# Layer norm by features from the fourth group on, and probabilities turned with shared corners

## The chip, the cores and the metric

One core of a Trainium2 chip runs the kernel. Its engines work in order, each from a queue of its own, and are tied by semaphores: TensorE (PE) multiplies matrices, VectorE (DVE), ScalarE (ACT) and GpSimd (POOL) work element by element, SyncE (SP) issues the transfers (DMA). Matmuls write to PSUM; POOL sees SBUF alone. The metric is the device time of one execution in microseconds.

## The reference, cut to what matters

The input x has 32 sequences of 256 tokens with 128 features.

```python
xn = (x - mean(x)) / sqrt(var(x) + 1e-5)              # over the features of a token
h = relu(xn @ nm_w1 + nm_b1);  m = h @ nm_w2 + nm_b2
q, k, v = m @ q_w + q_b, m @ k_w + k_b, m @ v_w + v_b
# token s attends to tokens s-32 .. s+32 of its sequence
attn = softmax(q k^T / sqrt(128), over that band) v
# feed-forward: 16 experts, each token uses the 8 best, weights normalised and x 2.826
y = sum_e combine_e * ((silu(xn @ w_gate_e.T) * (xn @ w_up_e.T)) @ w_down_e.T)
y += (silu(xn @ shared_gate_w.T) * (xn @ shared_up_w.T)) @ shared_down_w.T
out = x + attn + y
```

## The kernel before

The 8192 tokens are worked in 16 groups of 512 (`GROUPS`), two sequences each. Within a group 17 steps (`STEPS`) run over the shared expert and the 16 others. All large tensors are held by features: 128 features on the partitions, 512 tokens along the row. Each float32 operand is kept as a high part and a low part of a type that TensorE takes at full speed, and a product is made of three matmuls (high x high, high x low, low x high; `PAIRS3`).

Each engine's program is the same double loop, group g and slot s, written out by hand. `slot(g, par, s)` says what the engine issues there, in that order; nothing else sets the order. `when(g, s, fresh)` gives another slot in group 0. In one slot:

- PE: gate_proj of step s+1 (three matmuls), a piece of the attention (`att_early`), down of step s-3, `att_late`, up_proj of step s. gate_proj waits for the silu two steps before, up_proj for `h_lo` two steps before, since they share a PSUM bank.
- ACT: `h_hi` (high part of the product of step s-1), the silu of step s+1, a piece of the attention.
- POOL: silu of step s+1 times the routing weights (`silu_c`, from `comb_b`, the weights of all experts spread over the partitions). There is none for step 0, so slot 16 has none.
- DVE: `h_prod` of step s-1 (silu_c times the up product, in PSUM), a piece of the attention or of the routing (`att`), then `h_lo` of step s-1.

The layer norm of a group runs ahead of it. x is loaded by tokens (`load_x`, 128 tokens on the partitions, four tiles). DVE takes the moments (`moments`, `variance`; slots 12 and 14, two groups ahead), POOL the power -1/2 (`inverse_std`, slot 16), DVE subtracts and multiplies (`normalise`, four instructions in slot 0, one group ahead). PE turns the result tile by tile into PSUM (`turn` into bank[1], slot 1), ACT copies the high part from there (`xn_hi`, slot 1) and DVE subtracts it for the low part (`xn_lo`, slot 2). The gate matmuls of the routing (`gate`) need both in slot 4. x is also loaded by features as `xres` (`load_res`), for the sum at the end (`finish_group`, slot 3 of the group after).

The attention of a sequence works with two tiles of 128 queries, each of which sees a window of 160 keys (`WIN`). DVE takes the row maximum (`row_max`, slots 4 and 6), ACT the exponential, DVE multiplies by the inverse sum (`normalise_probs`, slots 6 and 8) into `prob_n`, a row of 256 keys for each tile with zeros outside the window. PE turns it (`turn_probs`, slots 7 and 9): two halves of keys by two tiles, four transposes. ACT and DVE copy the parts that are not zero (`halves`, windows of 160 queries for either half of the keys) as high and low parts (`prob_hi`, `prob_lo`), which `attend` uses in slots 13 and 14.

SP issues all transfers in its loop order: in slot 3 the store of the last output, xres and x, in slot 13 the store of the routing weights to memory (`store_comb`, which waits for DVE's last routing instruction) and their spread over the partitions in four blocks (`spread`).

Of the kernel before, what the change touches and what calls it, by code (L numbers as in the profile page):

```python
# [12 lines left out]
P = 128  # L13
# [8 lines left out]
STEPS = E + 1  # L22
HALF = 32
WIN = P + HALF
EPS = 1e-5
ROUTE_SCALE = 2.826
SCALE = float(P) ** -0.5
# [18 lines left out]
NH = 4  # L46


DVE_LO = (6, 8)


# [13 lines left out]
    return next(d for d in range(1, 2 * STEPS + 1) if order[(p - d) % (2 * STEPS)] == order[p])  # L65


def layer(nc, x, x_t, watt, watt_t, expert_bias, wexp, out_t, c_dram):
    ctx = ExitStack()
    with ctx:  # L70
        def sb(name, shape, dt=F32):
# [5 lines left out]
        def sem(name):  # L77
# [25 lines left out]
        mv = sb("mv", [P, TILES, 2])  # L103
        var_eps = sb("var_eps", [P, TILES])
        rstd = sb("rstd", [P, TILES])
        xn = sb("xn", [P, TILES, P])
        xn_t = [[sb(f"xn_hi{i}", [P, T], F32R), sb(f"xn_lo{i}", [P, T], F32R)] for i in range(2)]


# [9 lines left out]
        row_sum = sb("row_sum", [P, TILES])  # L119
        row_inv = sb("row_inv", [P, TILES])  # L120
        prob = sb("prob", [P, TILES, WIN])
        prob_n = sb("prob_n", [P, TILES, SEQ])
        p_t = [sb("p_hi", [P, NB, 2, SEQ], F32R), sb("p_lo", [P, NB, 2, WIN], F32R)]


# [30 lines left out]
        s_expw_in = [sem(f"expw_loaded{i}") for i in range(len(EXPW))]  # L156
        s_xin = [sem(f"x_loaded{i}") for i in range(2)]
        s_xres = [sem(f"xres_loaded{i}") for i in range(2)]
        s_const0 = sem("const_cleared")
        s_const1 = sem("const_band_low")  # L160
        s_const = sem("const_ready")
# [34 lines left out]
        s_y_out = sem("y_evacuated")  # L196
        s_stored = [sem(f"y_stored{i}") for i in range(2)]

        names = """bn aggr var_eps rstd xn xn_tp xn_hi xn_lo gate_mm gate_s gate_e
# [36 lines left out]
        def flat(t):  # L236
            return t[:].rearrange("p a d -> p (a d)")

        def halves(b):

            return b[:].rearrange("p (t c) -> p t c", t=2)[:, :, 0:WIN]

        @block.sync
        def _(sp):
            def load_x(g, par):
                sp.dma_start(xin[par][:], x[g * T:(g + 1) * T, :].rearrange("(a p) d -> p a d", p=P))\
                    .then_inc(s_xin[par], 16)
# [25 lines left out]
            def prologue():  # L273
                load_x(0, 0)
                sp.dma_start(att_raw[:], watt).then_inc(s_watt_in, 16)
                for i, (lo, hi) in enumerate(EXPW):
                    sp.dma_start(exp_raw[:, lo:hi, :], wexp[:, lo:hi, :]).then_inc(s_expw_in[i], 16)
                    if i == 0:
                        sp.dma_start(att_t[:], watt_t).then_inc(s_wt_in, 16)
                    if i == 1:  # L280
                        sp.dma_start(ebias[:], expert_bias.to_broadcast([P, E])).then_inc(s_ebias_in, 16)
                    if i == 2:
                        load_x(1, 1)
                load_res(0, 0)

                store_comb(0, 0)
                for c in range(1, NCHUNK):
                    spread(0, 0, c, True)

            def slot(g, par, s):  # L290
                if s == 3:
                    if not first(g):
                        store_y(g - 1, 1 - par)
                    if not last(g):
                        if not first(g):

                            sp.wait_ge(s_stored[1 - par], 8 * (g - 1 + (1 + par)))
                        load_res(g + 1, 1 - par)
                    if not last(g, 1):

                        sp.wait_ge(S["xn"], g + 1)
                        load_x(g + 2, par)
                if s == 13 and not last(g):
# [12 lines left out]
        def _(pe):  # L316
# [30 lines left out]

            def turn_probs(seq):
                dst = score_bank[seq]
                for kb in range(2):  # L350
                    for t in range(2):
                        c = kb * (SEQ - (P - HALF)) + t * P
                        done = nc.tensor.transpose(dst[:, c:c + P],  # L353
                                                   prob_n[:, 2 * seq + t, kb * P:(kb + 1) * P], ident[:])
                done.then_inc(S[f"pt{seq}"], 1)

            def attend(seq):
# [214 lines left out]
        def _(act):  # L572
# [6 lines left out]
                A(exp_w[0][:, s, :], exp_raw[:, s, :], ACT.Copy).then_inc(s_expw_hi, 1)  # L579

            def xn_hi(g, par):
                act.wait_ge(S["xn_tp"], g + 1)
                A(xn_t[par][0][:], bank[1][:], ACT.Copy).then_inc(S["xn_hi"], 1)

            def gate_exp(g):
                act.wait_ge(S["gate_s"], g + 1)
# [28 lines left out]

            def prob_hi(g, seq):
                act.wait_ge(S[f"pt{seq}"], g + 1)
                A(p_t[0][:, seq, :, 0:WIN], halves(score_bank[seq]), ACT.Copy).then_inc(S[f"p{seq}_hi"], 1)

            def gate_silu(g, par, s):  # L620
                i = (par + s) % 2
# [108 lines left out]
        def _(dve):  # L730
# [13 lines left out]
            def variance(g):  # L744
# [15 lines left out]

            def xn_lo(g, par):
                dve.wait_ge(S["xn_hi"], g + 1)
                V.tensor_tensor(xn_t[par][1][:], bank[1][:], xn_t[par][0][:].bitcast(F32), ALU.subtract)\
                    .then_inc(S["xn_lo"], 1)

            def gate_sum(g):
# [141 lines left out]
            def normalise_probs(g, seq):  # L908
# [2 lines left out]
                V.reciprocal(row_inv[:, n], row_sum[:, n]).then_inc(S[f"inv{seq}"], 1)  # L911
                dve.wait_ge(S[f"inv{seq}"], g + 1)
                for t in range(2):
                    c = t * (P - HALF)
                    done = V.tensor_scalar(prob_n[:, 2 * seq + t, c:c + WIN], prob[:, 2 * seq + t, :],
                                           row_inv[:, 2 * seq + t:2 * seq + t + 1], None, ALU.mult)
                done.then_inc(S[f"pn{seq}"], 1)

            def prob_lo(g, seq):
                dve.wait_ge(S[f"p{seq}_hi"], g + 1)  # L920
                V.tensor_tensor(p_t[1][:, seq, :, :], halves(score_bank[seq]),
                                p_t[0][:, seq, :, 0:WIN].bitcast(F32), ALU.subtract).then_inc(S[f"p{seq}_lo"], 1)

            def att(g, par, s):
                more = not last(g)
                more2 = not last(g, 1)
                if first(g):
                    fresh_att(s)
                if s == when(g, 0, 3) and more:
                    normalise(g + 1, 1 - par)  # L930
                if s == when(g, 1, 4):
                    hid_n_lo(g)
# [28 lines left out]
                if s == when(g, 12, 13) and more2:  # L961
                    moments(g + 2, par)
                if s == 14:
                    if more2:
                        variance(g + 2)
                    if more:
                        hid_lo(g + 1)
# [58 lines left out]
        def _(pool):  # L1026
# [6 lines left out]

            def inverse_std(g):
                pool.wait_ge(S["var_eps"], g + 1)
                G.tensor_tensor(rstd[:], var_eps[:], power[:], ALU.pow).then_inc(S["rstd"], 1)

            def prologue():
                G.memset(power[:], -0.5)
# [29 lines left out]
            def slot(g, par, s):  # L1069
# [16 lines left out]
                                    silu[i][:].rearrange("p (l x) -> p l x", l=2),  # L1086
                                    comb_b[:, :, s1 - 1, :], ALU.mult).then_inc(s_silu_c, 1)
                elif not last(g, 1):
                    inverse_std(g + 2)
# [42 lines left out]
```

## Time and profile before

| | us |
|---|---|
| median of 3 runs (lowest, highest) | 715.92 (715.48, 717.18) |
| the profiled execution | 715.54 |
| its span, first to last instruction | 713.4 |
| PE busy | 702.2 (98%) |
| DVE busy | 573.1 (80%) |
| ACT busy | 440.6 (62%) |
| POOL busy | 405.3 (57%) |

The span is what the profiler sees of the execution; 2.1 us lie around it. Busy time is the union of an engine's instructions. Matmuls overlap each other, so their durations do not add up to their share of the time; the distance from one start to the next does. In the rows below, a line of the code stands as L396, a tile group as ps_u<-xn_hi,exp_w_hi (written, then read), and "x4" behind a row says how many instructions it merges.

### The profile page before, as it was taken

The page shows a single profiled execution, that of the slowest core. Times are in us where ns is not written, and L with a number is a line of the kernel's source. Part 1 is how long each engine was busy: PE and PEld are TensorE (multiplying, and loading weights), DVE is VectorE, ACT ScalarE, POOL GpSimd, SP SyncE. Part 2 cuts the span into 40 slices and gives each one's busy share as a digit, 9 for nine tenths or more (in the row PEclk, how much of TensorE's full clock was granted, in tenths as well). Part 3 has the DMA queues.
Part 4 walks back from the last instruction along what each step waited for, and adds up shares of the span by engine and source line. Part 5 has one row for each costly group of instructions (what it writes and reads, how often), then busy time and mean ns, then how long its engine had stood idle before and what let it go on. Part 6 is the DMA issues. An engine that isn't in the chain of part 4 may idle for free.

```text
span 713.4 us, 10683 instructions
## 1 busy us (share of the span) xinstructions
PE 702.2 (98%) x3412; PEld 577.4 (81%) x3412; DVE 573.1 (80%) x1598; ACT 440.6 (62%) x878; POOL 405.3 (57%) x363
## 2 busy tenths in 40 slices
PE   8889999999999999999999999999999999999997
PEld 6668888888888888888888888888888888888886
DVE  6888787887878888788887878878788887878775
ACT  5766665656665576655657566566665766656573
POOL 4785665555556555666555555554656546555463
PEclk9999999999999999999999999999999999999999
DMA  7606144071621506134061421516125061430600
GB/s 260 208 0 221 62 129 154 5 247 33 206 77 46 228 10 239 45 109 175 2 236 45 178 104 35 219 30 237 46 79 203 2 236 45 150 117 8 247 0 16
DMA packets 36519, 83.67 MB, mean 117 GB/s; under 512 B 7152, under 2 KB 15600, under 8 KB 36464
## 3 DMA queue, kind: packets, MB, share of 16 engines
q1 hardware_dynamic: 36464, 83.00, 33.7%
q8 instruction: 27, 0.44, 0.3%
q14 instruction: 28, 0.23, 0.1%
HBM read 78.27 MB, written 4.72 MB: 116 GB/s over the span
## 4 chain that ended last, share of the span: by engine, by line
PE 94%; DVE 3%; ACT 2%; issue 0%; DMA 0%; POOL 0%; DVEq 0%
PE ps_y L406 26%; PE ps_u L396 26%; PE ps_g L386 26%; PE bank L321 3%; PE bank L363 3%; PE bank L344 3%; PE bank L326 2%; PE bank L353 2%; PE bank L333 2%; PE ps_y L372 1%; DVE ps_u L997 1%; DVE h_lo L1003 1%; ACT h_hi L631 0%; DMA xin<-x 0%; DVE xn L755 0%
## 5 line engine op out<-in xcount | busy, mean ns | idle before, releaser
L1085 POOL TENSOR_TENSOR silu_c<-silu,comb_b 128x512 f32<-128x512 f32 x256 | 330.7, 1294 | 291.1 <-ACT silu L623 289.5
L631 ACT ACTIVATE h_hi<-ps_u 128x512 fp32r<-128x512 f32 x272 | 162.5, 597 | 258.4 <-DVE ps_u L997 256.4
L1003 DVE TENSOR_TENSOR h_lo<-ps_u,h_hi 128x512 fp32r<-128x512 f32 x272 | 185.8, 683 | 59.7 <-ACT h_hi L631 59.5
L997 DVE TENSOR_TENSOR ps_u<-silu_c,ps_u 128x512 f32<-128x512 f32 x256 | 176.9, 691 | 44.5 <-PE ps_u L396 38.7
L623 ACT ACTIVATE silu<-ps_g 128x512 f32<-128x512 f32 x272 | 161.5, 594 | 1.7 <-PE ps_g L386 1.5
L396 PE MATMUL ps_u<-xn_hi,exp_w_hi 128*128 128x512 f32 x272 | 110.5, 406 | 4.7 <-DVE h_lo L1003 4.7
L406 PE MATMUL ps_y<-h_hi,exp_w_hi 128*128 128x512 f32 x272 | 112.6, 414 | 0.4 <-DVE h_lo L1003 0.4
L386 PE MATMUL ps_g<-xn_hi,exp_w_hi 128*128 128x512 f32 x272 | 108.1, 397 | 0.0
L386 PE MATMUL ps_g<-xn_lo,exp_w_hi 128*128 128x512 f32 x272 | 107.8, 396 | 0.0
L386 PE MATMUL ps_g<-xn_hi,exp_w_lo 128*128 128x512 f32 x272 | 107.6, 396 | 0.0
L406 PE MATMUL ps_y<-h_hi,exp_w_lo 128*128 128x512 f32 x272 | 107.5, 395 | 0.0
L396 PE MATMUL ps_u<-xn_lo,exp_w_hi 128*128 128x512 f32 x272 | 107.4, 395 | 0.0
L406 PE MATMUL ps_y<-h_lo,exp_w_hi 128*128 128x512 f32 x272 | 107.2, 394 | 0.0
L396 PE MATMUL ps_u<-xn_hi,exp_w_lo 128*128 128x512 f32 x272 | 107.2, 394 | 0.0
L396 PEld LDWEIGHTS ps_u<-xn_hi,exp_w_hi 128*128 128x128 f32 x272 | 51.3, 189 | 16.2 <-DVE h_lo L1003 6.2
L386 PEld LDWEIGHTS ps_g<-xn_hi,exp_w_hi 128*128 128x128 f32 x272 | 51.3, 188 | 12.7 <-POOL exp_w_lo L1031 0.4
L386 PEld LDWEIGHTS ps_g<-xn_hi,exp_w_lo 128*128 128x128 f32 x272 | 51.3, 189 | 12.4
L406 PEld LDWEIGHTS ps_y<-h_hi,exp_w_lo 128*128 128x128 f32 x272 | 51.1, 188 | 12.5
L396 PEld LDWEIGHTS ps_u<-xn_hi,exp_w_lo 128*128 128x128 f32 x272 | 51.0, 188 | 12.1
L386 PEld LDWEIGHTS ps_g<-xn_lo,exp_w_hi 128*128 128x128 f32 x272 | 51.1, 188 | 12.0
L396 PEld LDWEIGHTS ps_u<-xn_lo,exp_w_hi 128*128 128x128 f32 x272 | 51.4, 189 | 10.1
L406 PEld LDWEIGHTS ps_y<-h_hi,exp_w_hi 128*128 128x128 f32 x272 | 51.3, 189 | 9.6 <-DVE h_lo L1003 0.8
(146 smaller groups left out, 992.1 us busy)
## 6 DMA issues: line engine op xcount, KB each, us to landing
comb_b<-c_dram SPq DMA_DIRECT2D x63, 1024.0 KB, 8.9
xin<-x SPq DMA_DIRECT2D x16, 256.0 KB, 3.4
xres<-x_t SPq DMA_DIRECT2D x16, 256.0 KB, 2.9
out_t<-xres SPq DMA_DIRECT2D x16, 256.0 KB, 2.0
exp_raw<-wexp SPq DMA_DIRECT2D x2, 960.0 KB, 10.8
c_dram<-comb_t SPq DMA_DIRECT2D x64, 8.0 KB, 1.8
exp_raw<-wexp SPq DMA_DIRECT2D x1, 768.0 KB, 7.6
exp_raw<-wexp SPq DMA_DIRECT2D x1, 384.0 KB, 5.4
```

The costliest lines, as they stand in the source:

```text
L321: done = mm(dst[:], att_w[a][:, w, :], parts[b][:], start=n == 0, stop=n == 2)
L326: done = nc.tensor.transpose(dst[:, a * P:(a + 1) * P], src[:, a * P:(a + 1) * P], ident[:])
L344: done = mm(dst[:, t * SEQ:t * SEQ + WIN], q_t[a][:, q0:q0 + P], hid_t[b][:, k0:k0 + WIN], start=n == 0, stop=n == 2)
L363: done = mm(bank[2][:, col:col + wide], hid_n[a][:, seq * 2 + kb, :], p_t[b][:, seq, kb, 0:wide], start=kb == 0 and n == 0, stop=kb == 1 a ...
L386: done = mm(ps_g[i][:], exp_w[a][:, s, 0:P], xn_t[par][b][:], start=n == 0, stop=n == 2)
L396: done = mm(ps_u[i][:], exp_w[a][:, s, P:2 * P], xn_t[par][b][:], start=n == 0, stop=n == 2)
L406: done = mm(ps_y[:], exp_w[a][:, s, 2 * P:3 * P], h_t[i][b][:], start=s == 0 and n == 0, stop=s == STEPS - 1 and n == 2, skip_group_check= ...
L623: A(silu[i][:], ps_g[i][:], ACT.Silu).then_inc(s_silu, 1)
L631: A(h_t[hbuf(par, s)][0][:], ps_u[(par + s) % 2][:], ACT.Copy).then_inc(s_h_hi, 1)
L997: V.tensor_tensor(ps_u[i][:], src[:], ps_u[i][:], ALU.mult).then_inc(s_h, 1)
L1003: V.tensor_tensor(t[1][:], ps_u[(par + s) % 2][:], t[0][:].bitcast(F32), ALU.subtract)\
L1085: G.tensor_tensor(silu_c[i][:].rearrange("p (l x) -> p l x", l=2), silu[i][:].rearrange("p (l x) -> p l x", l=2), comb_b[:, :, s1 - 1, :], ...
```

## The change

Two parts.

Layer norm. For groups 3 to 15 (`TURNED = 3`) x is loaded by tokens (now with four neighbouring tokens on a partition) for the moments alone, and once more by features, straight into `xn`. The mean and the inverse deviation of the 512 tokens are stored to memory and read back spread over all partitions (`mom_b`, 2 x 512 per partition). POOL then subtracts the mean in two halves (slots 14 and 15) and multiplies (slot 16), two groups ahead. `xn_hi` and `xn_lo` read `xn` in SBUF. The instructions of `normalise` on DVE and of `turn` on PE are gone for these groups. The moments are taken three groups ahead in slots 12 and 13, the power goes to slot 7, `xn_lo` for all groups but the first to slot 3. SP gets load_turned in slot 5 and, in slot 8, the store of the moments, the wait for it, and the spread.

Probabilities. `prob_n` holds one row of 384 per sequence: the first tile's window in columns 0 to 159, the second's in 224 to 383. PE turns it in three blocks of 128. The middle block holds the first tile's keys 128 to 159 and the second tile's keys 96 to 127; a query of the other tile has zeros at those keys, so one block serves both windows, which now lie 224 apart.

```diff
+APART = 3 * P - WIN
+TURNED = 3
         xn = sb("xn", [P, TILES, P])
+        mom = sb("mom", [P, 2, TILES])
+        mom_b = sb("mom_b", [P, 2, T])
-        prob_n = sb("prob_n", [P, TILES, SEQ])
+        prob_n = sb("prob_n", [P, NB, 3 * P])
-        def halves(b):
-            return b[:].rearrange("p (t c) -> p t c", t=2)[:, :, 0:WIN]
+        def windows(b):
+            return b[:, 0:2 * APART].rearrange("p (t c) -> p t c", t=2)[:, :, 0:WIN]
 # SP
+            def load_turned(g):
+                if g == TURNED:
+                    sp.wait_ge(S["xn_tp"], g)
+                else:
+                    sp.wait_ge(S["xn_lo"], g)
+                sp.dma_start(flat(xn), x_t[:, g * T:(g + 1) * T]).then_inc(s_xt, 16)
+            def spread_moments(g):
+                n = g - TURNED + 1
+                sp.wait_ge(S["rstd"], g + 1)
+                sp.wait_ge(S["mean"], n)
+                sp.dma_start(st_dram.rearrange("k (p a) -> p k a", p=P), mom[:]).then_inc(s_mom_st, 16)
+                sp.wait_ge(s_mom_st, 16 * n)
+                if n > 1:
+                    sp.wait_ge(S["xn"], g)
+                sp.dma_start(mom_b[:], st_dram.rearrange("(o k) t -> o k t", o=1).to_broadcast([P, 2, T]))\
+                    .then_inc(s_mom_b, 16)
                 if s == 3: ...
+                if s == 5 and TURNED <= g + 2 < GROUPS:
+                    load_turned(g + 2)
+                if s == 8:
...
+                    if TURNED <= g + 2 < GROUPS:
+                        spread_moments(g + 2)
 # PE
             def turn_probs(seq):
                 dst = score_bank[seq]
-                for kb in range(2):
-                    for t in range(2):
-                        c = kb * (SEQ - (P - HALF)) + t * P
-                        done = nc.tensor.transpose(dst[:, c:c + P],
-                                                   prob_n[:, 2 * seq + t, kb * P:(kb + 1) * P], ident[:])
+                for n in range(3):
+                    done = nc.tensor.transpose(dst[:, n * P:(n + 1) * P], prob_n[:, seq, n * P:(n + 1) * P],
+                                               ident[:])
-                if s == when(g, 1, 5) and more:
+                if s == when(g, 1, 5) and g + 1 < TURNED:
                     pe.wait_ge(S["xn"], g + 2)
 # DVE
             def variance(g):
...
+                if g > TURNED:
+                    dve.wait_ge(S["rstd"], g)
                 V.tensor_scalar(var_eps[:], mv[:, :, 1], EPS, None, ALU.add).then_inc(S["var_eps"], 1)
+                if g >= TURNED:
+                    n = g - TURNED
+                    if n > 0:
+                        dve.wait_ge(s_mom_st, 16 * n)
+                    V.tensor_copy(mom[:, 0, :], mv[:, :, 0]).then_inc(S["mean"], 1)
-                if s == when(g, 0, 3) and more:
+                if s == when(g, 0, 3) and g + 1 < TURNED:
                     normalise(g + 1, 1 - par)
-                if s == when(g, 2, 6) and more:
+                if s == when(g, 3, 6) and more:
                     xn_lo(g + 1, 1 - par)
+                if s == 12 and TURNED < g + 3 < GROUPS:
+                    moments(g + 3, 1 - par)
+                if s == 13: ... variance(g + 3)
 # POOL
             def inverse_std(g):
                 pool.wait_ge(S["var_eps"], g + 1)
+                if g > TURNED:
+                    pool.wait_ge(s_mom_st, 16 * (g - TURNED))
+                dst = rstd[:] if g < TURNED else mom[:, 1, :]
+                G.tensor_tensor(dst, var_eps[:], power[:], ALU.pow).then_inc(S["rstd"], 1)
+            def centre(g, half):
+                n = g - TURNED + 1
+                if half == 0:
+                    pool.wait_ge(s_xt, 16 * n)
+                    pool.wait_ge(s_mom_b, 16 * n)
+                c = slice(half * T // 2, (half + 1) * T // 2)
+                G.tensor_tensor(flat(xn)[:, c], flat(xn)[:, c], mom_b[:, 0, c], ALU.subtract)\
+                    .then_inc(S[f"centred{half}"], 1)
+            def normalise(g):
+                n = g - TURNED + 1
+                pool.wait_ge(S["centred0"], n)
+                pool.wait_ge(S["centred1"], n)
+                G.tensor_tensor(flat(xn), flat(xn), mom_b[:, 1, :], ALU.mult).then_inc(S["xn"], 1)
                 elif not last(g, 1):
+                    if g + 2 < TURNED: inverse_std(g + 2)
+                    else: normalise(g + 2)
+                if TURNED <= g + 2 < GROUPS:
+                    if s == 7: inverse_std(g + 2)
+                    if s == 14: centre(g + 2, 0)
+                    if s == 15: centre(g + 2, 1)
```

## Rows read from the trace of the kernel before

**Rows 1.** The page: busy time and share of each engine, instructions.

```profile
PE 702.2 (98%) x3412; PEld 577.4 (81%) x3412; DVE 573.1 (80%) x1598; ACT 440.6 (62%) x878; POOL 405.3 (57%) x363
```

**Rows 2.** Engines' busy time in one group's stretch; PEclk is the granted clock.

```profile
79.30:122.30 43.00, 43.00 (x211) 35.53 (x211) 35.09 (x100) 26.68 (x54) 24.28 (x21) 1.00 0.35 117
```

**Rows 3.** Timeline of POOL: start, length, what, [idle before <-who ended it].

```profile
331.27 1.35 POOL L1066 TENSOR_SCALAR mask_k<-mask,key_term 128x160 f32<-128x160 f32 x2
...
343.44 2.54 POOL L1085 TENSOR_TENSOR silu_c<-silu,comb_b 128x512 f32<-128x512 f32 x2 [4.31 <-ACT silu L623]
346.81 1.28 POOL L1085 TENSOR_TENSOR silu_c<-silu,comb_b 128x512 f32<-128x512 f32 x1 [0.82 <-ACT silu L623]
...
362.38 1.30 POOL L1085 TENSOR_TENSOR silu_c<-silu,comb_b 128x512 f32<-128x512 f32 x1 [1.46 <-ACT silu L623]
363.64 1.04 POOL L1036 TENSOR_TENSOR rstd<-var_eps,power 128x4 f32<-128x4 f32 x1
367.76 1.29 POOL L1085 TENSOR_TENSOR silu_c<-silu,comb_b 128x512 f32<-128x512 f32 x1 [3.09 <-ACT silu L623]
...
386.48 2.54 POOL L1085 TENSOR_TENSOR silu_c<-silu,comb_b 128x512 f32<-128x512 f32 x2 [4.31 <-ACT silu L623]
```

**Rows 4.** The waits: in total, times, longest.

```profile
PE ps_u L396 <- DVE h_lo L1003: 4.7, 4, 1.6
```

**Rows 5.** Timeline of PE, turning of xn in group 7.

```profile
326.07 0.60 PE L326 MATMUL bank<-ident,xn 128*128 128x128 f32 x4
...
326.74 0.40 PE L406 MATMUL ps_y<-h_lo,exp_w_hi 128*128 128x512 f32 x1
```

**Rows 6.** Groups of instructions: busy us, mean ns | idle before.

```profile
L326 PE MATMUL bank<-ident,xn 128*128 128x128 f32 x60 | 9.0, 272 | 0.0
```

**Rows 7.** Timeline of PE, a turning of probabilities.

```profile
304.30 0.60 PE L353 MATMUL bank<-ident,prob_n 128*128 128x128 f32 x4
...
304.97 0.39 PE L396 MATMUL ps_u<-xn_lo,exp_w_hi 128*128 128x512 f32 x1
```

**Rows 8.** Timeline of group 0, DVE, POOL and PE.

```profile
42.96 1.57 DVE L915 TENSOR_SCALAR prob_n<-prob,row_inv 128x160 f32<-128x160 f32 x2
...
43.42 1.01 POOL L1031 TENSOR_TENSOR exp_w_lo<-exp_raw,exp_w_hi 128x384 fp32r<-128x384 f32 x1
...
44.45 0.68 DVE L1003 TENSOR_TENSOR h_lo<-ps_u,h_hi 128x512 fp32r<-128x512 f32 x1
...
45.19 0.50 PE L396 MATMUL ps_u<-xn_hi,exp_w_hi 128*128 128x512 f32 x1 [1.12 <-DVE h_lo L1003]
...
52.73 0.50 PE L396 MATMUL ps_u<-xn_hi,exp_w_hi 128*128 128x512 f32 x1 [1.40 <-DVE h_lo L1003]
```

**Rows 9.** Timeline of DVE in group 7, slots 3, 5 and 8.

```profile
332.45 0.69 DVE L1003 TENSOR_TENSOR h_lo<-ps_u,h_hi 128x512 fp32r<-128x512 f32 x1 [0.66 <-ACT h_hi L631]
...
335.93 0.70 DVE L997 TENSOR_TENSOR ps_u<-silu_c,ps_u 128x512 f32<-128x512 f32 x1 [0.83 <-PE ps_u L396]
...
345.64 0.65 DVE L915 TENSOR_SCALAR prob_n<-prob,row_inv 128x160 f32<-128x160 f32 x2
...
346.53 0.67 DVE L1003 TENSOR_TENSOR h_lo<-ps_u,h_hi 128x512 fp32r<-128x512 f32 x1
```

**Rows 10.** Timeline of PE in group 7, slots 4 and 9.

```profile
333.45 0.18 PE L333 MATMUL bank<-gate_w,xn_hi 128*128 128x32 f32 x1
...
347.69 0.48 PE L396 MATMUL ps_u<-xn_hi,exp_w_hi 128*128 128x512 f32 x1
```

**Rows 11.** The page: transfers, KB each, median us to landing.

```profile
comb_b<-c_dram SPq DMA_DIRECT2D x63, 1024.0 KB, 8.9
...
c_dram<-comb_t SPq DMA_DIRECT2D x64, 8.0 KB, 1.8
```

**Rows 12.** Timeline of group 0, slot 2, POOL and DVE.

```profile
21.85 1.01 POOL L1036 TENSOR_TENSOR rstd<-var_eps,power 128x4 f32<-128x4 f32 x1
...
22.07 0.68 DVE L823 TENSOR_TENSOR hid_lo<-hid,hid_hi 128x512 fp32r<-128x512 f32 x1
```

More of the change, by code:

```diff
@@ L65, in hdist, with layer @@
     return next(d for d in range(1, 2 * STEPS + 1) if order[(p - d) % (2 * STEPS)] == order[p])
-def layer(nc, x, x_t, watt, watt_t, expert_bias, wexp, out_t, c_dram):
+def layer(nc, x, x_t, watt, watt_t, expert_bias, wexp, out_t, c_dram, st_dram):
     ctx = ExitStack()
@@ L158, in layer @@
         s_xres = [sem(f"xres_loaded{i}") for i in range(2)]
+        s_xt = sem("x_t_loaded")
+        s_mom_st = sem("moments_stored")
+        s_mom_b = sem("moments_spread")
         s_const0 = sem("const_cleared")
@@ L197, in layer @@
         s_stored = [sem(f"y_stored{i}") for i in range(2)]
-        names = """bn aggr var_eps rstd xn xn_tp xn_hi xn_lo gate_mm gate_s gate_e
+        names = """bn aggr var_eps rstd mean centred0 centred1 xn xn_tp xn_hi xn_lo gate_mm gate_s gate_e
             gate_1 score select top8 rest weight wsum winv comb comb_t
@@ L245, in load_x @@
             def load_x(g, par):
-                sp.dma_start(xin[par][:], x[g * T:(g + 1) * T, :].rearrange("(a p) d -> p a d", p=P))\
-                    .then_inc(s_xin[par], 16)
+                rows = x[g * T:(g + 1) * T, :]
+                rows = rows.rearrange("(a p) d -> p a d" if g < TURNED else "(p a) d -> p a d", p=P)
+                sp.dma_start(xin[par][:], rows).then_inc(s_xin[par], 16)
+            def load_turned(g):
[14 more added lines that the diff above has]
+                    .then_inc(s_mom_b, 16)
             def load_res(g, par):
@@ L298, in slot @@
                         load_res(g + 1, 1 - par)
-                    if not last(g, 1):
+                    if first(g):
                         sp.wait_ge(S["xn"], g + 1)
                         load_x(g + 2, par)
+                    elif not last(g, 2):
+                        if g + 1 < TURNED:
+                            sp.wait_ge(S["xn"], g + 2)
+                        else:
+                            sp.wait_ge(S["bn"], g + 2)
+                        load_x(g + 3, 1 - par)
+                if s == 5 and TURNED <= g + 2 < GROUPS:
+                    load_turned(g + 2)
+                if s == 8:
+                    if first(g):
+                        sp.wait_ge(S["xn"], g + 2)
+                        load_x(g + 3, 1 - par)
+                    if TURNED <= g + 2 < GROUPS:
+                        spread_moments(g + 2)
                 if s == 13 and not last(g):
@@ L581, in xn_hi @@
             def xn_hi(g, par):
-                act.wait_ge(S["xn_tp"], g + 1)
-                A(xn_t[par][0][:], bank[1][:], ACT.Copy).then_inc(S["xn_hi"], 1)
+                if g < TURNED:
+                    act.wait_ge(S["xn_tp"], g + 1)
+                else:
+                    act.wait_ge(S["xn"], g + 1)
+                A(xn_t[par][0][:], bank[1][:] if g < TURNED else flat(xn), ACT.Copy).then_inc(S["xn_hi"], 1)
             def gate_exp(g):
@@ L617, in prob_hi @@
                 act.wait_ge(S[f"pt{seq}"], g + 1)
-                A(p_t[0][:, seq, :, 0:WIN], halves(score_bank[seq]), ACT.Copy).then_inc(S[f"p{seq}_hi"], 1)
+                A(p_t[0][:, seq, :, 0:WIN], windows(score_bank[seq]), ACT.Copy).then_inc(S[f"p{seq}_hi"], 1)
             def gate_silu(g, par, s):
@@ L762, in xn_lo @@
                 dve.wait_ge(S["xn_hi"], g + 1)
-                V.tensor_tensor(xn_t[par][1][:], bank[1][:], xn_t[par][0][:].bitcast(F32), ALU.subtract)\
+                src = bank[1][:] if g < TURNED else flat(xn)
+                V.tensor_tensor(xn_t[par][1][:], src, xn_t[par][0][:].bitcast(F32), ALU.subtract)\
                     .then_inc(S["xn_lo"], 1)
@@ L913, in normalise_probs @@
                 for t in range(2):
-                    c = t * (P - HALF)
-                    done = V.tensor_scalar(prob_n[:, 2 * seq + t, c:c + WIN], prob[:, 2 * seq + t, :],
+                    c = t * APART
+                    done = V.tensor_scalar(prob_n[:, seq, c:c + WIN], prob[:, 2 * seq + t, :],
                                            row_inv[:, 2 * seq + t:2 * seq + t + 1], None, ALU.mult)
@@ L920, in prob_lo @@
                 dve.wait_ge(S[f"p{seq}_hi"], g + 1)
-                V.tensor_tensor(p_t[1][:, seq, :, :], halves(score_bank[seq]),
+                V.tensor_tensor(p_t[1][:, seq, :, :], windows(score_bank[seq]),
                                 p_t[0][:, seq, :, 0:WIN].bitcast(F32), ALU.subtract).then_inc(S[f"p{seq}_lo"], 1)
@@ L960, in att @@
                     route_weights(g + 1, 1 - par)
-                if s == when(g, 12, 13) and more2:
-                    moments(g + 2, par)
+                if g == TURNED - 2:
+                    if s == 4:
+                        moments(g + 2, par)
+                    if s == 5:
+                        variance(g + 2)
+                if s == 12 and TURNED < g + 3 < GROUPS:
+                    moments(g + 3, 1 - par)
+                if s == 13:
+                    if first(g):
+                        moments(g + 2, par)
+                    elif g + 3 < GROUPS:
+                        variance(g + 3)
                 if s == 14:
-                    if more2:
+                    if first(g):
                         variance(g + 2)
@@ L1035, in inverse_std @@
                 pool.wait_ge(S["var_eps"], g + 1)
-                G.tensor_tensor(rstd[:], var_eps[:], power[:], ALU.pow).then_inc(S["rstd"], 1)
+                if g > TURNED:
[15 more added lines that the diff above has]
+                G.tensor_tensor(flat(xn), flat(xn), mom_b[:, 1, :], ALU.mult).then_inc(S["xn"], 1)
             def prologue():
@@ L1088, in slot @@
                 elif not last(g, 1):
-                    inverse_std(g + 2)
+                    if g + 2 < TURNED:
+                        inverse_std(g + 2)
+                    else:
+                        normalise(g + 2)
+                if TURNED <= g + 2 < GROUPS:
+                    if s == 7:
+                        inverse_std(g + 2)
+                    if s == 14:
+                        centre(g + 2, 0)
+                    if s == 15:
+                        centre(g + 2, 1)
                 if s == when(g, 2, 5):
@@ L1128 @@
     c_dram = nc.dram_tensor("c_dram", (2, 2 * E, 2, P), F32, kind="Internal").ap()
-    layer(nc, *args, out_t, c_dram)
+    st_dram = nc.dram_tensor("st_dram", (2, T), F32, kind="Internal").ap()
+    layer(nc, *args, out_t, c_dram, st_dram)
     r = run_bass_kernel_spmd(nc, [arrays], core_ids=[0])
```

## The prediction

> **What bounds the kernel now.** I read the page first. TensorE is busy for 98% of the span, while VectorE, the next engine, has 80% [rows 1]. So I ask where TensorE ever waits. From 79.30 to 122.30 us, which is one group of the loop, it is busy for 43.00 of 43.00 us at full clock [rows 2], and the same place of two groups lies 386.48 - 343.44 = 43.04 us apart [rows 3]: a stream of matmuls without a hole. The waits agree: the largest of TensorE is up_proj behind VectorE's h_lo, 4 times in the whole run, 4.7 us together [rows 4]. Hence an instruction taken out of TensorE's stream in a full group shortens the span by the time for which it holds the stream, as long as no other engine becomes late. The busy durations are not that time, since matmuls overlap; the distance between starts is.
>
> **What a transpose holds.** From the start of the four transposes of xn to the start of the second matmul behind them it is 326.74 - 326.07 = 0.67 us [rows 5]: the four, and the distance from one matmul to the next. The row of the transposes tells the two apart: 0.60 us for four, less the 0.272 us that one lasts [rows 6], is 0.33 us for three pitches, or 0.109 each. Four hold 0.44 us, and the 0.23 us left of the 0.67 is the matmul's. The turning of the probabilities gives 304.97 - 304.30 = 0.67 again, so I use 0.109 per transpose there too [rows 7].
>
> **The change, part by part.**
>
> *xn by features, no turning.* Groups 3 to 15, that is 13, lose four transposes each: 52 x 0.109 = 5.67 us. They all stand in slot 1 of groups 2 to 14, which are full ones.
>
> *Corners in one piece.* Each of the 32 turnings issues three transposes in place of four: 32 x 0.109 = 3.49 us. But group 0's two savings disappear in its stalls: TensorE waits 1.12 us for h_lo just ahead of the first and 1.40 us behind the second [rows 8], so that VectorE sets the pace there. I count 30: 3.27 us. The copies of the windows keep their size and number, so ACT and VectorE have the same work on them.
>
> *VectorE.* It loses the four multiply-subtracts of slot 0 and gains one copy of four columns. Slot 0 is not what TensorE waits for, so this is worth nothing by itself. The low part of xn moves from slot 2 to slot 3, where VectorE waited 0.66 us for ACT [rows 9]: it fits. It now reads two SBUF tensors. If it had to wait out the whole pair of mask instructions on POOL (1.35 us from 331.27, [rows 3]) it would end near 331.27 + 1.35 + 0.69 = 333.31; the gate matmuls that need it start at 333.45 [rows 10] or, with TensorE 0.44 us ahead, at 333.01. So its price is between 0 and 0.3 us a group. I take 0, nearest to the row of 0.66: only a loss of both handovers gives the other end. The moments move from slot 14 to 13 and belong to a later group; slot 14 is relieved by as much.
>
> *POOL.* New are two half-tile subtractions and one multiplication, and the power moves from slot 16 to slot 7. A full-tile product takes at most 1.30 us, and I bound a half by it. The first half comes into the 1.46 us of idle time ahead of 362.38; the product there ends at 363.68, then the second half and the multiplication end by 363.68 + 1.3 + 1.3 = 366.3, while the next product starts at 367.76 [rows 3]. Hidden, with 1.5 us to spare. The power in slot 7 starts behind the pair of products that ends at 343.44 + 2.54 = 345.98 and ends 1.04 us later, at 347.02. The next product started at 346.81, so it is 0.2 us late, which its reader, in VectorE's next slot, does not notice.
>
> *The trip through memory.* It begins when the power ends (347.02) and must be over for slot 14, about 361: 14 us. From below it is bounded by two transfers of the 8 KB kind, 3.6 us; from above by 1.8 + 8.9 us, the latter for a spread of twice the size [rows 11]. 10.7 is less than 14, so it costs nothing; I would guess 7. If the cover were gone, each microsecond beyond it and beyond POOL's 1.46 us of idle time would stop POOL. On SP's queue the store, the wait for it and the spread now stand ahead of the store of the routing weights. That one waits for VectorE's routing work, which ends in slot 11, four slots after the power, so SP is back by then; if the spread's bytes delay it by a microsecond, the first block of the spread weights, used at 367.76 [rows 3], still comes in time by about as much.
>
> **What is late next.** Behind ACT's two table loads VectorE runs late through slots 8 to 12, and this is the one place with little room. In group 7 h_lo of step 7 ends at 346.53 + 0.67 = 347.20 and TensorE starts the up_proj that needs it at 347.69: 0.49 us [rows 9, 10]. In group 0, where TensorE does wait, it starts at 45.19 after h_lo's end at 44.45 + 0.68 = 45.13 [rows 8]: 0.06 is the price of the semaphore, so 0.43 is to spare. That room is measured from slot 5, where VectorE still waits for TensorE (0.83 us at 335.93, [rows 9]), so all that is saved before it moves both engines. Between it and these slots only the two turnings of probabilities are shorter, 0.22 us. There remain 0.21 us: nothing stalls, but little would make it.
>
> **The sum.** 715.54 (the profiled execution: a span of 713.4 and 2.1 around it) - 5.67 - 3.27 = 706.60. The median of the runs shown is 0.38 us above that execution, so 707.0 us.
>
> **The rivals.**
>
> *A, the power holds VectorE's second multiply.* In slot 8 the two multiplies of the probabilities start at 345.64, the first waits for POOL's products to end at 345.98, and both are done at 346.29 [rows 3, 9]. Now the power is queued right behind those products. Group 0 has the same pattern: two multiplies take 1.57 us together instead of 0.65, because a product of 384 columns that started on POOL at 43.42 came between them; they end at 44.53, 0.10 us after it [rows 8]. If the power did that, the pair would end at 345.98 + 1.04 + 0.10 = 347.12, 0.83 us late, of which 0.21 is covered: 0.62 us in each of groups 1 to 13, 8.1 us, which gives 714.7, or 715.1 as a median. Against it: at 22.07 VectorE's hid_lo, which reads two SBUF tensors, starts 0.22 us into a power of 1.01 us and takes 0.68, no longer than its like [rows 12]. A power reads only eight columns and seems to hold nothing while it computes. Chance 0.13. The Trainium skill, "SBUF — State Buffer", section "Who interferes with whom", says that a VectorE instruction in a two-port mode and a GpSimd one exclude each other, and that the later one "fully blocks". By that rule the power holds the multiply for its whole length and the time is this rival's. The trace agrees for instructions that stream their columns; for the power it speaks against it, as far as a two-input instruction can tell.
>
> *B, part of the room is used up.* Delays of 0.1 to 0.4 us beyond the 0.21 in slots 8 to 12, from a multiply held while the power reads or a low part of xn held in slot 3 (0.3 us at most): over 13 groups 1.3 to 5 us, so 708.3 to 712. Chance 0.09.
>
> *C, the moments come late: slower.* POOL executes in order. Its subtraction in slot 14 waits for the spread, and behind it stands the product for step 16 that VectorE multiplies with. A trip longer than 14 us plus the 1.46 us of idle time delays it. To be slower by over 0.3% (about what a measurement of this kernel can tell from no change, 2.15 us) each of 13 groups would have to lose (8.9 + 2.15) / 13 = 0.85 us, so the trip would have to last over 16.3 us; at 16.5 us each loses 1.04 us and the time is 707.0 + 13.5 = 720.5. For it speaks that the store writes runs of 16 bytes, which no row shows; against it the bound of 10.7. Chance 0.03.
>
> *D, the turnings of xn were free,* because a hidden wait takes their place, for instance finish_group in slot 3. Then 3.27 us alone are saved: 712.6. Against it stands that no row shows a wait of TensorE there. Chance 0.03.
>
> **How the numbers follow.** The forecast has 0.72, with 706.2 to 708 as its own range. The range for 8 in 10 takes in B and leaves out A: 705.9 to 712. Faster by over 0.3% means under 713.8: 0.72 + 0.09 + 0.03 (D) + 0.01 of A = 0.85. Same: the rest of A, 0.12. Slower: C, 0.03.
>
> **What would show it.** A period of 43.04 - 0.44 - 0.22 = 42.38 us between groups, with TensorE busy in all of it, shows both savings right; over 42.5 us makes the forecast wrong. A multiply of about 1 us in slot 8, and an up_proj of slot 9 that waits for h_lo, is A. POOL waiting for a DMA in slot 14 is C. TensorE waiting in slots 2 to 4 is D or the held low part of xn. The distance between starts around the three transposes should be 0.67 - 0.11 = 0.56 us.

## The result, and the profile after

| | us |
|---|---|
| changed kernel, median of 4 runs (lowest, highest) | 704.49 (703.62, 705.41) |
| kernel before beside it, median | 715.80 |
| ratio | 0.984, 95% interval 0.9824 to 0.9856 |
| profiled execution, its span | 703.68, 701.9 |

The kernel became 11.3 us faster by the medians. The time lies 2.5 us below the forecast of 707.0 and below its range, which began at 705.9. The medians mix two kinds of execution 1.5 to 1.7 us apart, with a mean granted clock of 0.994 to 0.995 or of 0.996 to 0.998, and leave out one execution of e1_before_pad32 that took 1786.93 us. The two profiled executions, with 0.998 and 0.997, are 715.54 - 703.68 = 11.9 us apart. What was said of the transposes and of the waits holds in the main; what is missing in the sum is a gain of TensorE in matmuls that the change does not touch.

The page of the changed kernel, busy time by engine, and its transfers:

```profile
PE 690.3 (98%) x3328; PEld 568.6 (81%) x3328; DVE 564.3 (80%) x1559; ACT 439.2 (63%) x878; POOL 446.0 (64%) x402
...
comb_b<-c_dram SPq DMA_DIRECT2D x63, 1024.0 KB, 8.7
mom_b<-st_dram SPq DMA_DIRECT2D x13, 512.0 KB, 3.8
```

The instructions of TensorE fell by 84, the 52 and 32 transposes. POOL has 41 us more, VectorE 9 less [rows 1]. Now a whole group (columns as in [rows 2]):

```profile
121.20:163.40 42.20, 42.20 (x207) 34.93 (x206) 34.47 (x96) 26.64 (x54) 27.42 (x25) 1.00 0.41 138
```

TensorE is busy in all of it, as before, at the full level of its clock (1.00). Its timeline in slots 5 to 9 of group 7 (start, length, what):

```profile
332.83 0.40 PE L444 MATMUL ps_u<-xn_hi,exp_w_hi 128*128 128x512 f32 x1
...
337.00 0.40 PE L444 MATMUL ps_u<-xn_hi,exp_w_hi 128*128 128x512 f32 x1
...
342.21 0.49 PE L401 MATMUL bank<-ident,prob_n 128*128 128x128 f32 x3
342.46 0.48 PE L444 MATMUL ps_u<-xn_hi,exp_w_hi 128*128 128x512 f32 x1
342.77 0.40 PE L444 MATMUL ps_u<-xn_lo,exp_w_hi 128*128 128x512 f32 x1
```

From the start of the three transposes to the start of the second matmul behind them it is 342.77 - 342.21 = 0.56 us, where with four it was 0.67 [rows 7]: the 0.11 of the sum. The first two rows are what the sum lacks. Between them lie two steps, 18 matmuls of 512 columns and nothing else: 4.17 us. Before, the same place reads

```profile
337.80 0.40 PE L396 MATMUL ps_u<-xn_hi,exp_w_hi 128*128 128x512 f32 x1
...
342.00 0.39 PE L396 MATMUL ps_u<-xn_hi,exp_w_hi 128*128 128x512 f32 x1
```

4.20 us. On the mean an untouched matmul starts between 1 and 2 ns sooner, and a group has 153 in its steps alone. The gain is not spread evenly. The largest share lies at one place of the nine, between the second and the third matmul of gate_proj; before, and after:

```profile
340.83 0.40 PE L386 MATMUL ps_g<-xn_lo,exp_w_hi 128*128 128x512 f32 x1
341.07 0.40 PE L386 MATMUL ps_g<-xn_hi,exp_w_lo 128*128 128x512 f32 x1
...
335.85 0.39 PE L434 MATMUL ps_g<-xn_lo,exp_w_hi 128*128 128x512 f32 x1
336.07 0.39 PE L434 MATMUL ps_g<-xn_hi,exp_w_lo 128*128 128x512 f32 x1
```

Over the full groups this distance has a mean of 233 ns before and of 226 after; the other eight changed by between -4 and +1 ns each, 6 ns less in all. VectorE and POOL in slots 7 and 8 of the same group:

```profile
339.88 0.70 DVE L1067 TENSOR_TENSOR ps_u<-silu_c,ps_u 128x512 f32<-128x512 f32 x1 [0.27 <-POOL silu_c L1173]
340.48 0.16 DVE L971 RECIPROCAL row_inv<-row_sum 128x2 f32<-128x2 f32 x1
340.67 0.66 DVE L975 TENSOR_SCALAR prob_n<-prob,row_inv 128x160 f32<-128x160 f32 x2
341.26 0.39 DVE L846 MAX8 top<-select 128x8 f32<-128x16 f32 x4
341.57 0.67 DVE L1073 TENSOR_TENSOR h_lo<-ps_u,h_hi 128x512 fp32r<-128x512 f32 x1
```

```profile
338.47 2.55 POOL L1173 TENSOR_TENSOR silu_c<-silu,comb_b 128x512 f32<-128x512 f32 x2 [4.32 <-ACT silu L674]
340.97 1.05 POOL L1109 TENSOR_TENSOR mom<-var_eps,power 128x4 f32<-128x4 f32 x1
...
354.40 1.30 POOL L1173 TENSOR_TENSOR silu_c<-silu,comb_b 128x512 f32<-128x512 f32 x1 [0.83 <-ACT silu L674]
355.66 0.73 POOL L1117 TENSOR_TENSOR xn<-xn,mom_b 128x256 f32<-128x256 f32 x1
357.07 1.30 POOL L1173 TENSOR_TENSOR silu_c<-silu,comb_b 128x512 f32<-128x512 f32 x1 [0.68 <-ACT silu L674]
358.32 0.74 POOL L1117 TENSOR_TENSOR xn<-xn,mom_b 128x256 f32<-128x256 f32 x1
359.21 1.29 POOL L1124 TENSOR_TENSOR xn<-xn,mom_b 128x512 f32<-128x512 f32 x1
...
380.64 2.56 POOL L1173 TENSOR_TENSOR silu_c<-silu,comb_b 128x512 f32<-128x512 f32 x2 [4.32 <-ACT silu L674]
```

The power starts at 340.97, before the second multiply of the pair could, and the pair takes 0.66 as before. h_lo ends at 342.24 and up_proj starts at 342.46: of 0.49 us, 0.22 are left. The same place of two groups is 380.64 - 338.47 = 42.17 us apart; before it was 43.04, and the sum said 42.38.

### The profile page after: what moved, and what is told of

It reads as the page before. It is cut to its first block, busy times and chain, and to the rows that moved or that the text cites. A ratio compares the mean times of both kernels' runs of the same rounds, so it can differ in the third digit from the quotient of the medians.

```text
span 701.9 us, 10616 instructions
## 1 busy us (share of the span) xinstructions
PE 690.3 (98%) x3328; PEld 568.6 (81%) x3328; DVE 564.3 (80%) x1559; ACT 439.2 (63%) x878; POOL 446.0 (64%) x402
## 4 chain that ended last, share of the span: by engine, by line
PE 93%; DVE 3%; ACT 3%; issue 1%; DMA 0%; POOL 0%; DVEq 0%
PE ps_u L444 26%; PE ps_y L454 26%; PE ps_g L434 26%; PE bank L371 3%; PE bank L411 3%; PE bank L394 3%; PE bank L383 2%; PE ps_y L420 1%; PE bank L401 1%; PE bank L376 1%; DVE ps_u L1067 1%; DVE h_lo L1073 1%; ACT h_hi L682 1%; DMA xin<-x 0%; DVE xn L814 0%
## 5 line engine op out<-in xcount | busy, mean ns | idle before, releaser
L434 PE MATMUL ps_g<-xn_lo,exp_w_hi 128*128 128x512 f32 x272 | 106.0, 390 | 0.0
```

The costliest lines, as they stand in the source:

```text
L434: done = mm(ps_g[i][:], exp_w[a][:, s, 0:P], xn_t[par][b][:], start=n == 0, stop=n == 2)
```

## Experiments

The suspicion came from the addresses of the tiles. The starts below are worked out from the order and sizes of the tiles in the program, each start rounded up to 32 bytes; no trace holds an address, but how far an edit moves a tile does not hang on that rounding. The change puts `mom` and `mom_b` (32 and 4096 bytes per partition) ahead of xn_hi, and `prob_n` is 1024 bytes shorter. So xn_hi, xn_lo and everything behind them, h included, start 4128 or 3104 bytes further on: before they stood 32 bytes beyond a multiple of 64, now at one. The experts' weights, allocated earlier, stand at a multiple of 64 in both. Thirty-two unused bytes in the right place test this. The period is the distance between the same pair of POOL's products in full groups, the mean of 13 in the one profile of each kernel. From one group to the next it keeps within 0.02 us in the changed kernel and within 0.07 in the worst case (e6), and the granted clock is 1.00 there in all of them, so it tells these kernels apart better than the times. All are measured against the kernel before; its median was 715.7 to 715.9.

| kernel | start mod 64: weights, xn, h | period, us | median, us | ratio (95%) |
|---|---|---|---|---|
| before | 0, 32, 32 | 43.03 | 715.8 | |
| e1_before_pad32 | 0, 0, 0 | 42.86 | 713.07 | 0.9955 (0.9938, 0.9971) |
| e13_before_weights32 | 32, 32, 32 | 42.88 | 713.63 | 0.9972 (0.9961, 0.9983) |
| e3_corners_only | 0, 32, 32 | 42.81 | 712.47 | 0.9946 (0.9932, 0.9961) |
| e4_norm_only | 0, 0, 0 | 42.43 | 707.17 | 0.9881 (0.9861, 0.9900) |
| changed | 0, 0, 0 | 42.18 | 704.49 | 0.9840 (0.9824, 0.9856) |
| e2_after_pad32 | 0, 32, 32 | 42.37 | 707.05 | 0.9870 (0.9854, 0.9887) |
| e5_xn_off | 0, 32, 0 | 42.36 | 706.15 | 0.9870 (0.9853, 0.9887) |
| e7_weights_off | 32, 0, 0 | 42.35 | 706.19 | 0.9867 (0.9852, 0.9882) |
| e8_plus64 | 0, 0, 0 | 42.20 | 703.89 | 0.9837 (0.9821, 0.9852) |
| e9_all_off | 32, 32, 32 | 42.20 | 704.54 | 0.9836 (0.9819, 0.9854) |
| e6_h_off | 0, 0, 32 | 42.13 | 703.61 | 0.9828 (0.9814, 0.9843) |
| e10_h_apart | 32, 32, 0 | 42.12 | 704.05 | 0.9823 (0.9804, 0.9843) |
| e11_hold | 0, 0, 0 | 42.93 | 713.33 | 0.9968 (0.9953, 0.9983) |
| e12_from_group2 | 0, 0, 32 | 42.13 | 707.88 | 0.9886 (0.9860, 0.9911) |

**The placing, in the kernel before and in the changed one.**

```diff
+        pad = sb("pad", [P, 8])                 # e1 in the kernel before, e2 in the changed one
         xn_t = [[sb(f"xn_hi{i}", [P, T], F32R), sb(f"xn_lo{i}", [P, T], F32R)] for i in range(2)]
```

> The kernel before with one change: an unused tile of 32 bytes per partition ahead of xn_hi and xn_lo, so that they and every tile behind them (hid, q, z, prob_n, comb_b, silu, h) start 32 bytes later in SBUF, at a multiple of 64 instead of at 32 beyond one. Nothing else moves. Theory (placing of the tiles that TensorE streams): each 512-column matmul starts about 1.3 ns sooner, the group period falls from 43.03 to 42.86 us and the time by about 2.6 us, to 713.3. Rival (what VectorE and POOL do beside TensorE changed its pitch, or the order of work): nothing changes, 43.03 us and 715.9.

> The changed kernel with the same 32 bytes ahead of xn_hi and xn_lo, which puts these tiles and all behind them back to 32 beyond a multiple of 64. Theory (placing): the period rises from 42.18 to about 42.36 us, the time by 2.6 us to about 707.0, which is the forecast. Rival (work beside TensorE): stays at 42.18 us and 704.5.

Measured: 42.86 and 713.07 for the first, 42.37 and 707.05 for the second. 32 idle bytes give the kernel before 0.17 us a group and take 0.19 from the changed one, which then lands on the forecast (42.38 and 707.0). In e1 the distance inside gate_proj named above falls from 233 to 225 ns, in e2 it is back at 234. POOL's pair of products in two groups of the first:

```profile
342.43 2.55 POOL L1086 TENSOR_TENSOR silu_c<-silu,comb_b 128x512 f32<-128x512 f32 x2 [4.32 <-ACT silu L624]
...
385.29 2.55 POOL L1086 TENSOR_TENSOR silu_c<-silu,comb_b 128x512 f32<-128x512 f32 x2 [4.32 <-ACT silu L624]
```

**Each part alone.** The corners in the kernel before, and the changed kernel with the old `prob_n` and four transposes:

```diff
-                for kb in range(2):
-                    for t in range(2): ...      # four transposes
+                for n in range(3): ...          # three; e3 adds this to the kernel before, e4 takes it back
```

> The kernel before with the second part of the change alone: prob_n as rows of 384, three transposes in place of four. Tiles behind prob_n move by 1024 bytes, so their place within 64 bytes stays. By the sum: period 43.03 - 0.22 = 42.81 us, time 715.9 - 3.3 = 712.6. If the corners were what changed the matmuls' pitch, 42.65 us and 710.

> The changed kernel with the old probabilities (rows of 256, four transposes): the first part of the change alone, tiles at multiples of 64. By the sum plus placing: period 43.03 - 0.44 - 0.17 = 42.42 us, time 715.9 - 5.7 - 2.6 = 707.6. If placing is nothing and the pitch changed by the corners, 42.59 us and 710.2.

Measured: 42.81 and 712.47, 42.43 and 707.17. The corners are worth 0.22 us a group and leave the pitch (the distance from one matmul's start to the next) alone; the norm part is worth 0.60, which is 0.43 of transposes if e1's 0.17 is taken for the placing.

**Which tiles.** All four are the changed kernel with unused bytes in other places:

```diff
+        pad0 = sb("pad0", [P, 8])   # ahead of xn_hi, and again behind xn_lo: e5; ahead of h_hi: e6
+        pad0 = sb("pad0", [P, 8])   # ahead of exp_raw, and again ahead of ident: e7
+        pad0 = sb("pad0", [P, 16])  # ahead of xn_hi: e8
```

> The changed kernel with 32 unused bytes ahead of xn_hi and xn_lo and 32 behind them: these four tiles alone start 32 beyond a multiple of 64, all behind them are at multiples again. They are streamed by six of the nine matmuls of a step. Theory (the place of the streamed tile within 64 bytes sets its matmul's pitch): two thirds of the loss, period 42.18 + 0.12 = 42.30 us, time 704.5 + 1.8 = 706.3. Rival (it is the engines that write the other tiles, or the place of h): 42.18 us, 704.5.

> The changed kernel with 32 unused bytes ahead of the h tiles alone, which the three down matmuls of a step stream. Theory (place of the streamed tile): a third of the loss, period 42.18 + 0.06 = 42.24 us, time 705.4. Rival (the place of xn alone counts): 42.18 us, 704.5.

> The changed kernel with the experts' weights (raw, high, low) 32 bytes further on, at 32 beyond a multiple of 64, and everything streamed at multiples of 64. Theory (streamed tiles): 42.18 us and 704.5, as before the edit. Rival (the place of the weights relative to the streamed tiles counts, and the 32 bytes only happened to bring them together): the loss comes back, 42.36 us and 707.1.

> The changed kernel with 64 unused bytes ahead of xn_hi and xn_lo, so that they and all behind them move by 64 and keep their place within 64 bytes. Theory (the place within 64 bytes alone counts): 42.18 us, 704.5. Rival (a larger pattern of addresses, 128 bytes or more, or how the tiles lie to each other): some other period, in either direction by up to 0.2 us, up to 3 us in time.

Measured, in this order: 42.36 and 706.15, 42.13 and 703.61, 42.35 and 706.19, 42.20 and 703.89. My theory of the streamed tile failed. Moving the weights costs as much as moving xn (42.35 against 42.36), where it said nothing would happen; moving xn costs the whole loss and not two thirds of it; and moving h does not cost a third but gains 0.05. A shift by 64 bytes leaves the period as it was to 0.02 us (e8). So it is not a tile's own place but how xn lies to the weights it is streamed through, and that can be told apart by moving both.

```diff
+        pad0 = sb("pad0", [P, 8])               # e9: ahead of exp_raw
         exp_raw = sb("exp_raw", [P, STEPS, 3 * P])
...
+        pad1 = sb("pad1", [P, 8])               # e10 has this too, ahead of h_hi
```

> The changed kernel with 32 unused bytes ahead of the raw weights and nothing else: weights, xn, h and all tiles in between start 32 beyond a multiple of 64. Theory (only the place of the weights relative to the tiles that are streamed through them counts, mod 64): back to 42.18 us a group and 704.5. Rival (any of the two off a multiple costs, each for itself): at least as slow as with xn or the weights alone off, 42.36 us and 706.2 or more.

> The same, with another 32 bytes ahead of the h tiles, so that weights and xn are off and h at multiples of 64, the mirror image of the run with h alone off. Theory (relative place): its mirror, 42.15 us and 703.6. Rival (absolute place): slower than 706.

Measured: 42.20 and 704.54, 42.12 and 704.05. With weights and xn both at 32 beyond, the period is back to 0.02 us. The same in the kernel before, with no part of the change in it:

```diff
+        pad0 = sb("pad0", [P, 8])               # ahead of exp_raw, and pad1 ahead of ident
         exp_raw = sb("exp_raw", [P, STEPS, 3 * P])
```

> The kernel before with the experts' weights (raw, high, low) 32 bytes further on and another 32 bytes behind them: weights go to 32 beyond a multiple of 64, where xn, h and the rest already are (they move by 64 and keep their place within it). Theory (place of the weights relative to the streamed tiles): the same gain as from moving the streamed tiles to the weights, period 43.03 - 0.18 = 42.85 us and time 713.1. Rival (multiples of 64 are good in themselves, so leaving one costs): 43.03 us or more, 715.8 or more.

Measured: 42.88 and 713.63; the weights moved to the tiles give what the tiles moved to the weights gave. Two groups of e7 and two of e9 (POOL):

```profile
339.32 2.55 POOL L1175 TENSOR_TENSOR silu_c<-silu,comb_b 128x512 f32<-128x512 f32 x2 [4.32 <-ACT silu L676]
...
381.66 2.56 POOL L1175 TENSOR_TENSOR silu_c<-silu,comb_b 128x512 f32<-128x512 f32 x2 [4.31 <-ACT silu L676]
```

```profile
340.04 2.56 POOL L1174 TENSOR_TENSOR silu_c<-silu,comb_b 128x512 f32<-128x512 f32 x2 [4.32 <-ACT silu L675]
...
382.24 2.55 POOL L1174 TENSOR_TENSOR silu_c<-silu,comb_b 128x512 f32<-128x512 f32 x2 [4.32 <-ACT silu L675]
```

42.34 and 42.20. In both the weights stand at 32 beyond; in e7 xn and h do not, in e9 they do.

**The room in slots 8 to 12, and rival A's price.**

```diff
                     if s == 7:
+                        G.tensor_tensor(junk[:], exp_raw[:, 0, :], exp_raw[:, 1, :], ALU.subtract)
                         inverse_std(g + 2)
```

> The changed kernel with one instruction more on POOL in slot 7 of groups 1 to 13, right behind the pair of products and ahead of the power: a subtraction of 384 columns into a tile that nothing reads. Theory (an instruction that streams its columns holds VectorE's second multiply for its length, as in group 0, where the power does not): the second multiply takes 1.0 to 1.1 us instead of 0.29, VectorE's h_lo is 0.8 us late, TensorE has 0.16 us of room and waits 0.6 us for it in each of the 13 groups: period 42.8 us, time 704.5 + 8 = 712.5. Rival (the multiply goes ahead of it, or the room is larger): 42.2 us and 704.5.

POOL, VectorE and TensorE in group 7:

```profile
342.80 2.54 POOL L1174 TENSOR_TENSOR silu_c<-silu,comb_b 128x512 f32<-128x512 f32 x2 [4.32 <-ACT silu L675]
345.30 1.02 POOL L1184 TENSOR_TENSOR junk<-exp_raw 128x384 f32<-128x384 f32 x1
346.28 1.03 POOL L1110 TENSOR_TENSOR mom<-var_eps,power 128x4 f32<-128x4 f32 x1
```

```profile
345.00 1.41 DVE L976 TENSOR_SCALAR prob_n<-prob,row_inv 128x160 f32<-128x160 f32 x2
346.34 0.40 DVE L847 MAX8 top<-select 128x8 f32<-128x16 f32 x4
346.66 0.67 DVE L1074 TENSOR_TENSOR h_lo<-ps_u,h_hi 128x512 fp32r<-128x512 f32 x1
```

```profile
347.38 0.50 PE L445 MATMUL ps_u<-xn_hi,exp_w_hi 128*128 128x512 f32 x1 [0.35 <-DVE h_lo L1074]
```

The pair of multiplies takes 1.41 us instead of 0.66, ending 0.09 after the subtraction, h_lo ends at 347.33 and TensorE starts 0.05 later, after a wait. The period is 42.93, 0.75 us more than in the changed kernel, and the time 8.8 us more, near the 8 expected: 0.60 us are lost ahead of the up_proj of slot 9, and another 0.10 ahead of that of slot 11, where VectorE was still behind.

**A try for a better version.**

```diff
-TURNED = 3
+TURNED = 2      # h_hi 32 bytes on, too; variance(2) leaves slot 14 of group 0 for slot 5
```

> A try for a better version: h tiles 32 bytes on, and the layer norm by features from group 2 instead of 3, so that group 1 loses its four transposes too. By the sum: 703.6 - 0.44 = 703.2. Against it: group 0, in which VectorE and POOL set the pace, gets 0.9 and 0.7 us more of VectorE in slots 4 and 5 and 3.8 us more of POOL; if none of it is covered, 704.5 or more.

It fell short: 707.88 (706.33 to 710.21). Its full groups are like those of e6 (42.13), and group 1 loses its four transposes, but the beginning grew: the first matmul of group 1 starts at 65.90 us, against 63.44 in e9, whose granted clock in the first 36 us was the same (0.90 from 12 to 36 us), and 61.98 in e6 (0.95). The engines' busy times late in group 0 (the window ends in group 1), first e12, then e6:

```profile
36.00:79.00 43.00, 39.01 (x186) 31.15 (x187) 37.16 (x99) 27.41 (x56) 33.68 (x33) 1.00 0.34 118
```

```profile
36.00:79.00 43.00, 40.12 (x202) 32.92 (x202) 37.32 (x109) 27.03 (x55) 31.48 (x30) 1.00 0.35 123
```

TensorE has 1.1 us less, POOL 2.2 us more; how much of the loss is POOL's and how much VectorE's was not told apart. The lowest median is e6's, 703.61. Its interval overlaps that of the changed kernel, so only the period (42.13 against 42.18, 0.75 us in 15 groups) says that it is faster, and e10 with 42.12 cannot be told from it.

## Why the prediction was wrong

- **What bounds the kernel: right.** TensorE without a hole in full groups, before and after.
- **What a transpose holds: right.** 0.22 us a group for the corners in e3, to the last digit; 0.60 less 0.17, that is 0.43, for the four of xn in e4 against 0.44. In total 13 x 0.66 + 2 x 0.22 = 9.0 us, for 8.9 in the sum.
- **The sum: here it failed.** "715.54 - 5.67 - 3.27" takes for granted that an instruction that stays keeps its pitch. It did not: 43.03 - 42.86 = 0.17 us a group, 2.6 us in 15 groups, for the sake of 32 bytes. Group 0 took 0.2 us more: group 1's first matmul starts at 62.02 instead of 61.84. So -9.0 - 2.6 + 0.2 = -11.4, and the span fell by 11.5. Another 0.3 us lies outside the span, of which 1.8 us instead of 2.1 are left; the sum took these for unchanged as well. The change's new tiles stood in the diff, and their sizes with them; I had read them for room, not for the place of what comes behind them. The range, too, had no case in which TensorE itself becomes faster, so it was narrow on the side where the time fell.
- **Group 0's two savings hidden: not shown apart.** Over nine kernels with the same work in group 0 group 1's first matmul starts at 61.8 to 62.1 us in six and at 63.2 to 63.4 in three (e2, e9, e10), which hides 0.2 us. The three had a granted clock of 0.89 to 0.90 from 12 to 36 us, the six 0.93 to 0.95; from 36 us on it is 1.00 in all.
- **POOL's new work and the trip: right.** The halves took 0.73, not the bound of 1.3. The trip was 7 us: power's end at 342.02, a store of 2.3 us by its median, a spread issued at 345.3 that lands 3.8 us later; it is used at 355.66.
- **The low part of xn in slot 3: right, by another row.** It took 0.69 us at once. The first of POOL's two mask instructions beside it, which began 0.06 us before it by the record, took 1.22 us instead of 0.69:

```profile
326.57 1.88 POOL L1154 TENSOR_SCALAR mask_k<-mask,key_term 128x160 f32<-128x160 f32 x2
```

```profile
326.62 0.69 DVE L823 TENSOR_TENSOR xn_lo<-xn,xn_hi 128x512 fp32r<-128x512 f32 x1
```

  That makes 1.88 us for the pair instead of 1.35 [rows 3], and the period shows no loss by it.
- **What is late next: right.** 0.21 us of room were forecast and 0.22 - 0.06 = 0.16 are there. What took the other 0.05 stays open: in e3, with the corners alone, 0.27 - 0.06 = 0.21 are left as forecast, but e2 has 0.16 as well, and its matmuls are the slow ones.
- **Rival A: rejected, and its price confirmed.** The power does not hold the multiply, an instruction that streams 384 columns does. The Trainium skill's rule ("SBUF — State Buffer", "Who interferes with whom"), that the later of the two is fully blocked, holds here for e11's instruction; it does not hold for the power, an instruction of 1.05 us with four columns, beside which the second multiply takes 0.29 us. B, C and D did not happen: a period of 42.18 is below the 42.38 of the sum.

## What to carry to other kernels

When TensorE runs without a hole, look at where the tiles lie as well as at what is issued: a new small tile moves all that come behind it, and here 32 bytes were worth 0.4% in either direction. Try an idle pad ahead of the streamed tiles before giving a small gain or loss to a change's logic, and compare the distance between the same places of two groups: here it repeats to a few hundredths of a microsecond where the time of a run spreads over one or two. For the rest, price what leaves a saturated engine by the distance between starts, and measure the room of the engine behind it from the last place where it waits.

## What the runs showed of the hardware

- A stream of matmuls of 512 float32 columns runs faster when the streamed tile xn and the weights lie alike within 64 bytes (both at a multiple, or both 32 beyond) than when they lie 32 apart: 0.15 to 0.18 us a group in e1, e5, e7 and e13, which is 1.0 to 1.2 ns for each of the 153 matmuls on the mean. It is no equal gain of each: the distance from gate_proj's second matmul to its third is 232 to 234 ns in every kernel with the two apart and 225 to 229 ns in every one with them alike, the largest difference at any of the nine places. For h the sign was the other way (0.05 us in e6 and 0.08 in e10 better when apart), and with xn apart its place made 0.01 (e5 against e2). Why the two differ stays open, and so does the reason for either: the hi and lo halves and the three parts of the weights were not moved one by one, and no distance but 32 and 64 bytes was tried. All these kernels keep the rule of the Trainium skill's "SBUF — State Buffer", section "Operand start alignment", that an operand starts at a multiple of its element's size; what differs here is speed alone.
- A VectorE multiply that waits while POOL's product runs gets in at the product's end, though POOL's next instruction starts there too (e11: product's end 345.34, multiply's end 345.44). The next multiply is then held by that POOL instruction if it streams 384 columns (e11: 1.41 us for the pair), and not if it computes a power of four (0.66 us).
- With a granted clock of 0.89 to 0.90 from 12 to 36 us group 1 began 1.1 to 1.6 us later than with 0.93 to 0.95 (one profile each of nine kernels with the same group 0). The distance between full groups, at 1.00 in all, does not show it.
